# Attention of three layers: row maxima of two heads in one VectorE instruction

## The reference

```
q, k, v = project(x), project(ctx), project(ctx)     # not in layer 2
scores  = einsum('bdhn,bdhm->bhnm', q, k) / sqrt(head_dim)
prob    = softmax(scores, axis=-1)                   # 256 x 256 for each head
out     = einsum('bhnm,bdhm->bdhn', prob, v)
```

## Time and profile before

| | us |
|---|---|
| median of 3 executions | 2522.51 (2516.19 to 2522.55) |
| profiled execution | 2525.09 |
| its span, first to last instruction | 2523.3 |
| busy: PE, DVE, ACT, POOL | 2034.0, 1814.2, 1403.7, 1186.2 |

### The profile page before, as it was taken

The page is one execution under the profiler, slowest core; times in us unless marked ns, Lnnn a source line. Parts: engine busy times, 40 slices in busy tenths (PEclk is TensorE's granted clock), DMA queues, the critical chain, the costliest instruction groups (busy, mean ns, idle before and its releaser), DMA issues. The chain is left out here.

```text
span 2523.3 us, 42640 instructions
## 1 busy us (share of the span) xinstructions
PE 2034.0 (81%) x13467; PEld 1242.7 (49%) x13467; DVE 1814.2 (72%) x4020; ACT 1403.7 (56%) x3553; POOL 1186.2 (47%) x1393
## 2 busy tenths in 40 slices
PE   5999698996799999999999849837835437887487
PEld 2444265663567776777777646514412223333144
DVE  4899485665799999999998663368837756888254
ACT  0777422451688888888888713215634423677343
POOL 3444102443788888888887523276312204333100
PEclk9999779998999999999999959958866656899699
DMA  4466313782300000000000042379610025576100
GB/s 133 138 188 171 100 48 106 249 260 82 59 16 20 20 22 16 20 20 22 16 16 3 1 151 88 117 188 237 174 47 1 0 87 133 153 198 159 44 1 34
DMA packets 256886, 223.20 MB, mean 88 GB/s; under 512 B 36441, under 2 KB 237756, under 8 KB 256028
## 3 DMA queue, kind: packets, MB, share of 16 engines
q1 hardware_dynamic: 231932, 173.06, 24.3%
q0 software_dynamic: 12240, 32.39, 5.1%
q10 hardware_dynamic: 12496, 15.03, 1.8%
HBM read 141.98 MB, written 79.32 MB: 88 GB/s over the span
## 5 line engine op out<-in xcount | busy, mean ns | idle before, releaser
L844 ACT ACTIVATE a_PT<-bank 128x512 f32<-128x512 f32 x640 | 355.8, 602 | 148.7 <-PE bank L607 132.3
L734 DVE TENSOR_REDUCE a_nm<-bank 128x2 f32<-128x512 f32 x640 | 409.2, 683 | 35.1 <-PE bank L600 32.9
L600 PE MATMUL bank<-a_stack_k,a_stack_q 48*128 48x256 bf16 (+2 forms) x1280 | 263.2, 298 | 108.9 <-DVE a_nm L734 75.3
L2913 PE MATMUL bank<-f_w,f_zc 128*128 128x512 bf16 x1152 | 283.9, 383 | 22.8 <-DVE f_zc L3021 18.2
L3233 POOL TENSOR_TENSOR f_hr<-f_hr,half_pow 128x4 f32<-128x4 f32 x192 | 244.5, 1273 | 84.8 <-DVE f_hr L3030 84.6
L607 PE MATMUL bank<-a_stack_q,a_stack_k 51*128 51x256 bf16 (+2 forms) x1280 | 252.2, 287 | 8.6 <-ACT a_PT L844 8.0
L600 PEld LDWEIGHTS bank<-a_stack_k,a_stack_q 48*128 48x128 bf16 (+2 forms) x1280 | 91.7, 99 | 272.9 <-DVE a_nm L734 195.8
L3125 ACT ACTIVATE f_Pm<-bank,f_nmax 128x128 f32<-128x128 f32 x512 | 182.5, 382 | 73.5 <-DVE f_nmax L3045 73.5
L622 PE MATMUL bank<-a_PT,a_V 128*32 128x256 f32 x2560 | 188.3, 416 | 1.4 <-ACT a_PT L844 1.4
L2913 PEld LDWEIGHTS bank<-f_w,f_zc 128*128 128x128 bf16 x1152 | 112.2, 99 | 123.0 <-issue 25.4
L3222 POOL TENSOR_TENSOR f_cf<-f_cbr,f_cmr 128x516 f32<-128x516 bf16 x128 | 157.0, 1226 | 12.6 <-DVE f_cb L3070 11.0
(11 more groups left out here) (370 smaller groups left out, 4721.2 us busy)
## 6 DMA issues: line engine op xcount, KB each, us to landing
cut<-a_parts SPq DMA_DIRECT2D x96, 192.0 KB
cut<-a_parts SPq DMA_DIRECT2D x144, 128.0 KB
o<-a_O SPq DMA_DIRECT2D x32, 512.0 KB
a_stack_q<-cut SPq DMA_DIRECT2D x64, 192.0 KB
a_stack_k<-cut SPq DMA_DIRECT2D x64, 192.0 KB
m_w<-in_w SPq DMA_DIRECT2D x32, 368.0 KB
moe_out<-m_oe ACTq DMA_DIRECT2D x32, 256.0 KB
a_num<-o SPq DMA_DIRECT2D x48, 128.0 KB
```

What stands on the lines that cost most here:

```text
L600: x = t.matmul(ps[:, n * D:(n + 1) * D], self.stack_q[rows, i, slot, n * P:(n + 1) * P], self.stack_k[rows, i, slot, :], start=True, stop= ...
L734: v.tensor_reduce(self.nm[:, g % 2, :, at % self.J, at // self.J], self.k.bank[h % 3][:, :].rearrange("p (n m) -> p n m", n=2), AX.X, ALU. ...
L844: a.activation(self.PT[:, h % 8, :, :].rearrange("p m n -> p (m n)"), self.k.bank[3 + h % 3][:, :], ACT.Exp).then_inc(self.a_exp.sem, 1)
L2913: x = t.matmul(ps[:, :], self.zc[:, b % 2, j, c_, :], self.fp8.w3[:, m, c_, at:at + BANK], start=(m == 0 and c_ == 0), stop=(m == 2 and c_ ...
```

## The change

The eight banks become one PSUM tensor, so that an access may cross from a bank to the next. First scores rotate over banks 0 to 3, in pairs of heads: TensorE signals after the odd head of a pair and waits before the even one, for the maxima of the pair two before. DVE takes the maxima of a pair in one instruction over 128 x 1024, at the odd step, and does nothing for them at the even one. Second scores rotate over banks 4 and 5: TensorE waits for the exponentials of the head that it scored at step s-2. The layout of the maxima in SBUF is unchanged. GpSimd waits for four pairs in place of eight heads.

```diff
-        self.bank = [ctx.enter_context(nc.psum_tensor(f"bank{i}", [P, BANK], F32)) for i in range(8)]
+        self.psum = ctx.enter_context(nc.psum_tensor("bank", [P, 8 * BANK], F32))
+        self.bank = [self.psum[:, i * BANK:(i + 1) * BANK] for i in range(8)]
+    def two_banks(self, n):
+        return self.psum[:, 2 * n * BANK:2 * (n + 1) * BANK]
...
-            if h >= 3:
-                t.wait_ge(self.v_max.sem, self.v_max.at(h - 2))
+            if h >= 4 and h % 2 == 0:
+                t.wait_ge(self.v_max.sem, self.v_max.at(h // 2 - 1))
...
-            if w >= 3:
-                t.wait_ge(self.a_exp.sem, self.a_exp.at(w - 2))
+            if w >= 2:
+                t.wait_ge(self.a_exp.sem, self.a_exp.at(w - 1))
...
-                i, ps = h // self.heads % self.NST, self.k.bank[h % 3]
+                i, ps = h // self.heads % self.NST, self.k.bank[h % 4]
-                if n == 1:
+                if n == 1 and h % 2:
                     x.then_inc(self.p_S.sem, 1)
-                i, ps = w // self.heads % self.NST, self.k.bank[3 + w % 3]
+                i, ps = w // self.heads % self.NST, self.k.bank[4 + w % 2]
...
-            if 0 <= t < self.NH:
-                self.maximum(v, t)
+            if 0 <= t < self.NH and t % 2:
+                self.maxima(v, t // 2)
...
+    def maxima(self, v, pair):
+        h, J = 2 * pair, self.J
         g, at = divmod(h, 8)
+        v.wait_ge(self.p_S.sem, self.p_S.at(pair + 1))
         if g >= 2 and at == 0:
             v.wait_ge(self.g_nm.sem, self.g_nm.at(g - 1))
+        nm = self.nm[:, g % 2, :, :, at // 2:at // 2 + 1] if J == 2 else self.nm[:, g % 2, :, :, at:at + 2]
+        v.tensor_reduce(nm.rearrange("p n j h -> p (j h) n"), self.k.two_banks(h % 4 // 2).rearrange("p (h n m) -> p h n m", h=2, n=2),
                         AX.X, ALU.max, negate=True).then_inc(self.v_max.sem, 1)
...
-        a.activation(..., self.k.bank[3 + h % 3][:, :], ACT.Exp).then_inc(self.a_exp.sem, 1)
+        a.activation(..., self.k.bank[4 + h % 2][:, :], ACT.Exp).then_inc(self.a_exp.sem, 1)
...
-        g.wait_ge(self.v_max.sem, self.v_max.at(8 * n + 8))
+        g.wait_ge(self.v_max.sem, self.v_max.at(4 * n + 4))
```

More of the change, by code:

```diff
@@ L419, in signals @@
         self.p_m, self.v_m = claim("a_p_m", len(self.uses)), claim("a_v_m", len(self.by_dve))
-        self.p_S, self.v_max, self.p_T, self.a_exp = (claim(f"a_{n}", NH) for n in ("p_S", "v_max", "p_T", "a_exp"))
+        self.p_S, self.v_max = (claim(f"a_{n}", NH // 2) for n in ("p_S", "v_max"))
+        self.p_T, self.a_exp = (claim(f"a_{n}", NH) for n in ("p_T", "a_exp"))
         self.g_nm, self.a_nm = claim("a_g_nm", NH // 8), claim("a_a_nm", NH // 8)
@@ L727, in dve_parameters @@
             c.after()
-    def maximum(self, v, h):
+    def maxima(self, v, pair):
+        h, J = 2 * pair, self.J
         g, at = divmod(h, 8)
-        v.wait_ge(self.p_S.sem, self.p_S.at(h + 1))
+        v.wait_ge(self.p_S.sem, self.p_S.at(pair + 1))
         if g >= 2 and at == 0:
             v.wait_ge(self.g_nm.sem, self.g_nm.at(g - 1))
-        v.tensor_reduce(self.nm[:, g % 2, :, at % self.J, at // self.J], self.k.bank[h % 3][:, :].rearrange("p (n m) -> p n m", n=2),
+        nm = self.nm[:, g % 2, :, :, at // 2:at // 2 + 1] if J == 2 else self.nm[:, g % 2, :, :, at:at + 2]
+        v.tensor_reduce(nm.rearrange("p n j h -> p (j h) n"), self.k.two_banks(h % 4 // 2).rearrange("p (h n m) -> p h n m", h=2, n=2),
                         AX.X, ALU.max, negate=True).then_inc(self.v_max.sem, 1)
@@ L843, in exponentials @@
             a.wait_ge(self.p_O.sem, self.p_O.at(h // 4 - 1))
-        a.activation(self.PT[:, h % 8, :, :].rearrange("p m n -> p (m n)"), self.k.bank[3 + h % 3][:, :], ACT.Exp).then_inc(self.a_exp.sem, 1)
+        a.activation(self.PT[:, h % 8, :, :].rearrange("p m n -> p (m n)"), self.k.bank[4 + h % 2][:, :], ACT.Exp).then_inc(self.a_exp.sem, 1)
     def copy_maxima(self, a, g):
```

## The result

The changed kernel takes 2574.81 us (median of 4 executions, 2566.11 to 2577.80) against 2522.07 for the kernel before: ratio 1.0209, 95% interval 1.0179 to 1.0239. It is 52.7 us slower. The way was forecast, the size was not: 2545.5 was predicted, and 2574.81 lies above the range's upper end of 2568.

The account below looks back on a forecast made before the run. A loop through PE, ACT and DVE was taken as the bound, not DVE's busy time. Layer 0 14 + layer 3 8 + stage ends 4 - layer 2 3 = 23 us longer, 2545.5 us in a median of runs; range 2508 to 2568.

Parts of the forecast that it names:

- What bounds the kernel: Attention stretches: a loop through PE, ACT and DVE sets the 14.36 us period of 16 heads, not DVE's busy time.
- Cost of a pair: DVE's maxima: a pair has 1.13 us from start to start against 1.20 for two singles, saving 0.065 us a pair.
- Step 11: PE in layer 0's batch item: starts 0.67 us later, waiting for step 9's exponentials queued behind ACT's copy of V.
- The pair behind X: Layer 0, maxima after DVE takes projection X: PE's step 6 0.47 us later, less 0.09 at step 1, net 0.38.
- Steady part of layer 0: Layer 0: 0.67 + 0.14 + 0.38 = 1.19 us a batch item, some 12 items, 14 us longer.
- Layer 3's seven steady items: Layer 3's batch items: 0.8 us longer each; twelve give 9.8, taken as 8 because stack loads hide some.
- The granted clock: PE's clock level: the prediction's sum had no term for a change in it.
- the ends of the stages: Layers 0 and 3, second scores only: 0.49 us per four heads, five groups each, 5 us, taken as 4.
- Layer 2: Layer 2's attention: the pairs' 0.065 us counts where DVE is busy, 3 us gained; bounds 10 gained to 8 lost.
- The third: Rival: the two-bank loop of 2.93 us per four heads binds everywhere, 63 us longer, 2585 us; chance 0.10.

Follow-up runs that it names:

- pairs in two reads: Changed kernel with each pair's maxima taken by two back-to-back instructions of 128 x 512 instead of one: 2581.41 us, ratio 1.0253.
- filler: Changed kernel with two extra fp32 matmuls of 128 columns ahead of PE's step 11 waits in layers 0 and 3: 2574.11 us, ratio 1.0195.
- projections later: Kernel before with DVE taking the projections C, X and Q one step later: 2505.62 us; the same edit on the changed kernel: 2557.11 us.
- Two banks only: Kernel before with only the second scores moved to two banks, first scores and maxima single over three banks: 2579.09 us, ratio 1.0232.
- the control: Kernel before with exponentials of only half of each bank (128 x 256), the products with the values reading that half twice: 2501.10 us, ratio 0.9906.

## Why the prediction missed

- **What bounds the kernel: right.** The loop through PE, ACT and DVE sets the period, not DVE's busy time. Of the page's 20.7 us less of DVE little counted (by "pairs in two reads" 0.12 us an item in layer 0, nothing in layer 3); one step's shift of the projections gave 16 to 20.
- **Cost of a pair: right,** 1.219 us and 1.13 from start to start. The Trainium skill (Perfetto Trace Analysis, Optimizing Scalar/DVE Operations) says that breaking instructions up may help where an engine that isn't saturated causes bubbles on others. The grouped kernel is slower, which agrees, but most of the loss is that of the banks: with single maxima over the same banks it is 8.4 us smaller. Of the about 125 ns an instruction that the Trainium skill gives in the same section, 0.065 us a pair were saved.
- **Step 11: the size was right, the cause wrong.** "The exponentials of step 9 stand in ACT's queue behind the copy of V" was put as the reason for 0.67 us. The copy was there, but moving it away left layer 0's period as it was and took 0.17 us off layer 3's. It is the round trip of 1.1 us over two banks.
- **The pair behind X: right.** 0.47 - 0.09 = 0.38 was forecast; step 6 comes 0.45 us later after step 1, and step 1 follows step 0 after 0.23 us in place of 0.31: 0.37.
- **Steady part of layer 0: right.** Items 3 to 13 are 13.6 us longer without the low clock; forecast 14. Layer 3's seven steady items are 0.83 longer each, forecast 0.8 (twelve of them are 9.6, not 9.8; nothing hangs on that). In its first six items another 5.0 us were lost, where the loads of stacks also show; forecast nothing.
- **The granted clock: the step that failed.** The sum holds no term for it, since the kernel before ran layer 0 at 1.00 up to 276 us: it was put at nothing without a reason why it should stay so under new waits of PE. In the profiled execution it cost 10.3 us in the middle of layer 0. "Five groups of four in layers 0 and 3 ... I take 4" for the ends of the stages became 6.1 (27.0 us behind the last maxima against 20.9) in layer 0 and 3.7 in layer 3. The loop over two banks was priced rightly there, 0.49 us a group at the low clock as worked out at the high one; where both kinds ran the end of layer 3 at 1.00, it took 20.7 us (filler) against 18.7 ("projections later" on the kernel before), 2.0 longer. What came on top, 4.1 and 1.7 us, goes with the clock: 0.62 and 0.59 behind the last maxima, 0.84 and 0.72 before. Together that is 16 of the 29 us that are missing.
- **The other 13 us.** The first items of layer 3 are 5, the last three items of layer 0 take 2.2 more, and the other stages 2.4. Layer 2 was forecast at -3 and measured at 0.1. Between its maxima 6.2 us were gained (10.2 us less of low clock there may be part of it), behind them 2.4 were lost, and 3.9 ahead of them. The 2.4 are a term that the sum left out: layer 2 has an end of the stage too (17.1 us before, 19.5 after, both at 1.00), five times 0.49.
- **The rivals.** The third, a two-bank loop everywhere, was priced at 2585 and is nearer in time. But it is not what happened: 15.55 us for 16 heads is 3.89 per four, far above its 2.93.

What stays open: what brings the low stretches, and so whether the changed kernel always has them. Each kernel has one profile. Kernels with two banks show from none to 41 us of them in layer 0, the two with three banks and the old order none, but "projections later" shows 10.2 and is the faster one all the same; its end of layer 0 ran at 0.59, with three banks. "Two banks only" lost 57 us with 3.4 of them, so the loss doesn't need them in the middle of layer 0; filling one wait of PE changed no time. What slows layer 3's first items and layer 2's start wasn't followed. Pairs together with three banks for the second scores (nine banks with the two in other use) weren't tried.

## What to carry to other kernels

A ring of n buffers between two engines allows a step each (round trip / n) us. Take the round trip from the timeline (here 0.46 + 0.60 + 0.06) and compare it with the fastest burst of the producer, not with its average period: PE's average step of 0.9 us hid that it does three in 0.45. Before merging instructions on a busy engine, look for idle time ahead of its other work; here moving that work by a step was worth 16 to 20 us, with the instructions as they were. Give a control every edit that its kernel has: moving DVE's work helped the kernel before as much as the changed one, so a comparison in which only one of them has it credits the order with a loss that it doesn't explain. And where a change puts waits ahead of PE, leave room in the forecast for its clock, also where the kernel before ran at 1.00.

## What was not expected of the hardware

- A stretch at the lower clock is dear: 10.2 us of it cost an item 3.65 us. In such a stretch the busy share of PE rises (97%) while the count of matmuls falls (72 against 117), so a busy share alone hides it and the clock's column shows it.
- One reduction over two adjacent PSUM banks costs the same as one over as many elements of SBUF: 1.219 us against 1.213.
- Halving the exponentials' elements took 21 us off the kernel before, though its steady period moved by 0.06 us: half of what the stages gained lies behind their last maxima. Part of that half is the clock and not the exponentials: the ends of layers 0 and 3 ran at 0.84 and 0.72 before and at 1.00 in the control, and at 1.00 the end of layer 3 takes 18.7 us with whole exponentials ("projections later"), 16.4 with half and 23.2 in the profile of before. The rest lies in the stages' first and last items and in layer 3's 0.21 us an item, and its cause wasn't followed.
